# Seams between the seven stretches of a three-layer graph network: leaving without a drain, early zero stores, early first groups

## What is computed

```python
# attention (the edges of edge_index are the first 25,000 by shape only; here all 50,000 are used, plus a loop for each node)
xl = (x @ Wl); xr = (x @ Wr)
e = leaky_relu(xl[src] + xr[dst]); logits = einsum(e, att)
alpha = softmax of logits over the edges of a node
out = segment_sum(alpha * xl[src], dst) + bias
y = elu(graph norm of out over all nodes)
x = layernorm(x + y)
# two relational layers
for l in range(2):
    msg = sum_b comp[l, b][etype] * (h[src] @ basis[l, b])
    h = tanh(segment_sum(msg, dst) + h @ loop_w[l] + bias[l])
x = layernorm(x + h)
```

## Time and profile before

| | us |
|---|---|
| median of 3 runs | 3581.94 (3573.18 to 3585.92) |
| the profiled execution | 3583.63 |
| its span, first to last instruction | 3581.8 |
| busy: PE, DVE, POOL, ACT | 2957.1, 2565.8, 2222.8, 1815.4 |
| ends of the seven stretches in it | 1160.3, 1516.5, 1827.6, 2369.5, 2649.7, 3191.9, 3581.0 |

### The profile page before, as it was taken

One profiled execution on the slowest core, in us unless ns is written; L12 is line 12 of the kernel. 1 busy time (PEld: TensorE's weight loads), 2 busy tenths in 40 slices (PEclk: granted clock), 3 DMA queues, 4 the chain that ended last, 5 costly groups with the idle time before them and its releaser, 6 DMA issues. The chain is left out here.

```text
span 3581.8 us, 65764 instructions
## 1 busy us (share of the span) xinstructions
PE 2957.1 (83%) x17251; PEld 2212.4 (62%) x17251; DVE 2565.8 (72%) x8027; ACT 1815.4 (51%) x4346; POOL 2222.8 (62%) x2605
## 2 busy tenths in 40 slices
PE   4787888878775788788869999969979999967776
PEld 4777777777774555477745555548855555545654
DVE  4777777777775798877757777734447777758887
ACT  2444444444442344389956666634436666635554
POOL 6777777777773122278877777712247777726666
PEclk9899898999887899999989999989989999989998
DMA  4455555444442788678823333359943333349886
GB/s 100 121 127 124 123 123 129 124 121 128 122 123 71 210 247 245 193 258 271 270 92 104 103 103 104 105 166 301 299 150 104 103 103 104 104 143 291 280 281 202
DMA packets 647622, 579.28 MB, mean 162 GB/s; under 512 B 74323, under 2 KB 534484, under 8 KB 647252
## 3 DMA queue, kind: packets, MB, share of 16 engines
q1 hardware_dynamic: 494436, 335.02, 31.6%
q0 software_dynamic: 82688, 207.65, 20.9%
q10 hardware_dynamic: 70128, 32.39, 3.3%
HBM read 366.34 MB, written 208.43 MB: 160 GB/s over the span
## 5 line engine op out<-in xcount | busy, mean ns | idle before, releaser
L1867 DVE SCALAR_TENSOR_TENSOR work<-bank,coef,work 128x128 f32<-128x128 f32 x2400 | 673.9, 342 | 244.7 <-ACT work L1308 241.0
L1032 PE MATMUL bank<-basis_s,work 128*128 128x512 f32 x1600 | 755.9, 595 | 1.5 <-ACT work L1301 1.5
L744 POOL DMA_INDIRECT work<-in_x_dram,slot_src x400 | 423.4, 1059 | 130.9 <-issue 121.6
L744 POOL DMA_INDIRECT work<-in_x_dram,slot_dst x400 | 417.8, 1045 | 122.0 <-issue 122.0
L793 POOL DMA_INDIRECT work<-h_d,slot_src x400 | 384.4, 961 | 132.0 <-issue 121.7
L793 POOL DMA_INDIRECT work<-x_d,slot_src x400 | 383.9, 960 | 132.0 <-issue 121.7
L1308 ACT ACTIVATE work<-bank,coef 128x128 f32<-128x128 f32 x800 | 294.1, 368 | 224.7 <-PE bank L1032 224.7
L1032 PEld LDWEIGHTS bank<-basis_s,work 128*128 128x128 f32 x1600 | 274.3, 191 | 196.6 <-issue 192.6
L758 POOL DMA_DIRECT2D conv_d<-work x99 | 74.0, 751 | 325.3 <-DVE work L1756 315.9
L1078 PE MATMUL bank<-work,loop_s 128*128 128x512 f32 x392 | 213.8, 627 | 73.5 <-ACT work L1349 73.4
L1043 PEld LDWEIGHTS bank<-work 128*126 128x126 f32 x1600 | 206.9, 189 | 101.6 <-issue 100.9
(11 more groups left out here) (273 smaller groups left out, 7835.4 us busy)
## 6 DMA issues: line engine op xcount, KB each, us to landing
w_d<-work SPq DMA_DIRECT2D x800, 62.5 KB
work<-in_x_dram SPq DMA_DIRECT2D x194, 256.0 KB, 3.1
work<-x_d SPq DMA_DIRECT2D x194, 256.0 KB, 4.0
w_d<-work SPq DMA_DIRECT2D x400, 66.9 KB
work<-w_d SPq DMA_DIRECT2D x398, 64.0 KB, 3.2
work<-w_d ACTq DMA_DIRECT2D x390, 64.0 KB, 3.3
xl_d<-work SPq DMA_DIRECT2D x97, 256.0 KB
work<-xl_d SPq DMA_DIRECT2D x97, 256.0 KB, 3.8
```

The lines of the kernel that those rows point to most:

```text
L744: pool.indirect_dma_start(quad(k, i % 3)[:, c, :], None, x, bass.IndirectOffsetOnAxis(ap=table[:, a:a + 1], axis=0)).then_inc(e_in[i % 3], 16)
L1032: pe.matmul(psum[YBANKS[k % 5]][:, :], quad(1, i % 2)[:, c, :], basis_s[:, l, :, :].rearrange("k b n -> k (b n)"), start=True, stop=True). ...
L1867: ins = dve.scalar_tensor_tensor(o, psum[YBANKS[k % 5]][:, b * D:(b + 1) * D], coef[:, i, l, c, b:b + 1], o, ALU.mult, ALU.add)
```

## The change

- `end_pool_stage` takes the place of `end_stage` for POOL at all seven places: POOL adds one to `stage_done` without a drain.
- The zeros past the end are made and stored at the beginning of stretches 1, 4 and 6 from `work[15]`, not at the end from `work[6]`; the wait for them stands before the first store of sums.
- `node_at` is worked out before the first join and not after it.
- Own rows of node groups 0 to 2 are loaded at the beginning of stretches 4 and 6; PE turns group 0, ACT copies it and DVE makes the one-hot matrices 0 and 1 before the bridges, within the stretch of edges. In `update` the product with `loop_w` stands ahead of the wait for the packed sums.
- The first three groups of stretch 3 are loaded at the end of stretch 2, when all of its groups are merged (`skip_rows` swaps its two buffers for that), and ACT computes one Exp right after the Sqrt of the graph norm.
- PE's wait for the weights stands after the transposes of the slots.

```diff
+        def end_pool_stage(k):
+            pool = nc.gpsimd
+            pool.sem_inc(stage_done, 1)
+            pool.wait_ge(stage_done, 5 * k)
...
             def save_sums(i):
                 sp.wait_ge(ec_cp, i + 1)
+                if i == 0:
+                    sp.wait_ge(zero_out, 16)
...
+            sp.wait_ge(zero_ok, 1)
+            end = addresses(sp, end_at[0:1, 0:1])[0]
+            sp.dma_start(w_d[0][bass.ds(end, P), :], work[15][:, 0:WIDE]).then_inc(zero_out, 16)
             for i in range(ROWS + 3):
...
-            sp.wait_ge(zero_ok, 1)
-            at = addresses(sp, end_at[0:1, 0:1])[0]
-            sp.dma_start(w_d[0][bass.ds(at, P), :], work[6][:, 0:WIDE]).then_inc(zero_out, 16)
-            sp.wait_ge(zero_out, 16)
             for k, c in enumerate(range(CHAINS - 1, 0, -1)):
...
-            for q in range(QUADS):
+            sp.wait_ge(r["m_ps"], QUADS - 2)
+            sp.wait_ge(cv_ok, PAIRS)
+            for q in range(3):
+                sp.wait_ge(r["nh_out"][q], 16)
+                load_nx(q)
+            end_stage(sp, 2)
+
+            for q in range(3, QUADS):
                 load_nx(q)
...
+                sp.dma_start(w_d[l + 1][bass.ds(end, P), :], work[15][:, 0:width]).then_inc(r["zero_out"], 16)
...
+                for q in range(3):
+                    load_own_rows(q)
+                sp.wait_ge(r["zero_out"], was["zero_out"] + 16)
                 for i in range(ROWS):
...
-            end_stage(pool, 1)
+            end_pool_stage(1)
...
             pe.wait_ge(consts, 12)
-            pe.wait_ge(weights_in, 16 * 10)
...
+            pe.wait_ge(weights_in, 16 * 10)
             pe.wait_ge(pos_ok, 1)
...
                 compact(ROWS - 1)
+                pe.wait_ge(r["t_cp"], was["t_cp"] + ROWS)
+                turn_nodes(0)
                 end_stage(pe, 4 + 2 * l)
...
-                    wait_packed(pe, l, q)
                     if q >= 3:
                         pe.wait_ge(r["th_ok"], was["th_ok"] + q - 2)
                     pe.matmul(to[:, 0:m], loop_s[:, l, :], work[7][:, (q % 2) * 512:(q % 2) * 512 + m],
                               start=True, stop=False, skip_group_check=True)
+                    wait_packed(pe, l, q)
...
             act.activation(stat[:, 5, :], stat[:, 4, :], ACT.Sqrt).then_inc(gn_std, 1)
+            act.activation(join[:, 7, :], ones[0:1, 0:H], ACT.Exp)
             end_stage(act, 2)
...
+                turned_nodes(0)
+                end_stage(act, 4 + 2 * l)
...
-                dve.memset(work[6][:, 0:width], 0.0).then_inc(r["zero_ok"], 1)
+                node_matrix(l, 0)
+                node_matrix(l, 1)
                 dve.wait_ge(r["c_cp"], was["c_cp"] + ROWS)
```

More of the change, by code:

```diff
@@ L640, in _, with load_own_rows @@
                 was, width = counts_before(l), D
+                sp.wait_ge(r["zero_ok"], was["zero_ok"] + 1)
+                end = addresses(sp, end_at[0:1, 0:1])[0]
+                sp.dma_start(w_d[l + 1][bass.ds(end, P), :], work[15][:, 0:width]).then_inc(r["zero_out"], 16)
+                def load_own_rows(q):
+                    for to, part in run_rows((x1_d, h1_d)[l], q, h_rows(q), True):
+                        sp.dma_start(to, part).then_inc(r["n_in"][q % RING], 16)
+                for q in range(3):
+                    load_own_rows(q)
+                sp.wait_ge(r["zero_out"], was["zero_out"] + 16)
                 for i in range(ROWS):
@@ L649, in _ @@
                     sp.wait_ge(r["w_out"][c], was["w_out"][c] + 16 * ROWS)
-                sp.wait_ge(r["zero_ok"], was["zero_ok"] + 1)
-                at = addresses(sp, end_at[0:1, 0:1])[0]
-                sp.dma_start(w_d[l + 1][bass.ds(at, P), :], work[6][:, 0:width]).then_inc(r["zero_out"], 16)
-                sp.wait_ge(r["zero_out"], was["zero_out"] + 16)
                 for k, c in enumerate(range(CHAINS - 1, 0, -1)):
@@ L667, in load_group @@
                     load_packed(sp, l, q, 0, 2)
-                    for to, part in run_rows((x1_d, h1_d)[l], q, h_rows(q), True):
-                        sp.dma_start(to, part).then_inc(r["n_in"][q % RING], 16)
+                    if q >= 3:
+                        load_own_rows(q)
                 def load_skip(q):
@@ L1045, in compact, with turn_nodes @@
                     last.then_inc(r["c_ps"], 1)
+                def turn_nodes(q):
+                    wait_own(pe, l, q)
+                    if q >= 2:
+                        pe.wait_ge(r["nt_cp"], was["nt_cp"] + q - 1)
+                    for t in range(quad_tiles(q)):
+                        rows = tile_rows(4 * q + t)
+                        last = pe.transpose(psum[q % 2][:, t * P:t * P + rows], h_rows(q)[0:rows, t, :], ident[0:rows, 0:rows])
+                    last.then_inc(r["nt_ps"], 1)
                 turn(0)
@@ L1058, in _ @@
                 compact(ROWS - 1)
+                pe.wait_ge(r["t_cp"], was["t_cp"] + ROWS)
+                turn_nodes(0)
                 end_stage(pe, 4 + 2 * l)
-                def turn_nodes(q):
-                    wait_own(pe, l, q)
-                    if q >= 2:
-                        pe.wait_ge(r["nt_cp"], was["nt_cp"] + q - 1)
-                    for t in range(quad_tiles(q)):
-                        rows = tile_rows(4 * q + t)
-                        last = pe.transpose(psum[q % 2][:, t * P:t * P + rows], h_rows(q)[0:rows, t, :], ident[0:rows, 0:rows])
-                    last.then_inc(r["nt_ps"], 1)
                 def update(q):
@@ L1608, in hot_types @@
                 last.then_inc(hot_ok, 1)
+            dve.memset(work[15][:, 0:WIDE], 0.0).then_inc(zero_ok, 1)
             for i in range(ROWS + 1):
@@ L1628, in _ @@
             dve.wait_ge(ec_cp, ROWS)
-            dve.memset(work[6][:, 0:WIDE], 0.0).then_inc(zero_ok, 1)
+            dve.wait_ge(tile_in, 16 * 4)
+            less, kept = (work[k][:, 0:512].rearrange("p (g w) -> p g w", g=4)[:, :, 0:TE] for k in (0, 1))
+            node_f = work[7][:, 0:4]
+            st.did(dve.tensor_tensor(less, node_row[:, :, 0:TE], tile_base[:, :].unsqueeze(2).to_broadcast([P, 4, TE]), ALU.is_lt))
+            st.did(dve.tensor_tensor(kept[:, :, 1:TE], node_row[:, :, 1:TE], node_row[:, :, 0:TE - 1], ALU.not_equal))
+            st.did(dve.memset(kept[:, :, 0:1], 1.0))
+            st.wait()
+            st.did(dve.tensor_tensor(less, less, kept, ALU.mult))
+            st.wait()
+            st.did(dve.tensor_reduce(node_f, less, AX.X, ALU.add))
+            st.wait()
+            st.did(dve.tensor_tensor(node_f, node_f, node_row[:, :, TE], ALU.add))
+            st.wait()
+            regions = work[7][:, 4:16].rearrange("p (c g) -> p c g", c=CHAINS - 1)
+            for c in range(1, CHAINS):
+                st.did(dve.tensor_scalar(regions[:, c - 1, :], node_f, chain_at[:, c:c + 1], float(GAP), ALU.is_ge, ALU.mult))
+            st.wait()
+            for c in range(1, CHAINS):
+                to = node_f if c < CHAINS - 1 else node_at[:, :]
+                st.did(dve.tensor_tensor(to, node_f, regions[:, c - 1, :], ALU.add))
+                st.wait()
             for k, c in enumerate(range(CHAINS - 1, 0, -1)):
@@ L1873, in term @@
                         ins.then_inc(r["y_used"], 1)
+                dve.memset(work[15][:, 0:width], 0.0).then_inc(r["zero_ok"], 1)
                 for k in range(-1, TILES_E):
```

37 lines of the change are left out of this document (5 added, 32 removed).

## The result

| | us |
|---|---|
| kernel before, median of 4 runs beside it | 3583.93 (3573.18 to 3585.95) |
| changed kernel, median of 4 runs | 3545.7 (3543.07 to 3546.76) |
| ratio, with its interval | 0.9898 (0.9877 to 0.9919) |
| span of the profiled execution, before and after | 3581.8 and 3543.2 |

The change gives 38.2 us where 42.3 were forecast. A second set of runs gave 0.9899 (0.9881 to 0.9917). Ends of stretches are read to 0.1 us, so a piece is good to about 0.1 us.

A forecast was written before the change was run, and what follows sets the result against it. Seven successive stretches were taken as paced by POOL (1, 4, 6), ACT (3), PE (5) and DMA (7). Gains 3.6 + 4.5 + 5.5 + 16.2 + 4.1 + 5.6 + 2.8 = 42.3 us gave 3540 us, range 3528 to 3557.

The forecast's parts named there:

- Start, 3.6 us: Program start: PE turns the slots without waiting for the weights, so POOL's first gather and stretch 1's end come 3.6 us earlier.
- End of stretch 1, 4.5: End of stretch 1: no zero store before the bridges (2.3 us) and SP last instead of DVE (2.2), 4.5 us.
- Seam 2 to 3, 5.5: Stretch 3's start: early loads and early table load bring the first Exp 5.9 us forward, taken as 5.5; ACT keeps it.
- The drains, 16.2: Ends of stretches 3 and 5: without POOL's drain each stretch ends 8.1 us earlier, 16.2 us together.
- Rival B: POOL's queue pays the 8.1 us before the first gathers of stretches 4 and 6 anyway; 3556 us, chance 0.12.
- Start of stretch 5, 5.6: Stretch 5's start: group 0 prepared early, first squash (tanh) at 2376.4 against 2382.05; PE keeps the 5.6 us.
- Start of stretch 7, 2.8: Stretch 7's start: DMA engines set the pace and save three groups' own rows, 2.8 us, bounds 2 and 5.6.
- The end, 0: Program end: without POOL's last drain the program's own drain takes the 8.1 us instead, so 0 us gained.
- Rival A: Program end: the end drain goes too, saving another 8.1 us; 3532 us, chance 0.15.
- Rival C: Drains go, but half of what stretches 3, 5 and 7 gain at their starts, 7 us, is given back; 3547 us, chance 0.15.
- Rival D: Gathers of stretches 4 and 6 run at stretch 1's slower pace, 78 us more; 3618 us, chance 0.03.
- Rival E: Little effect: Rival B with starts absorbed and zero stores in a new wait, within 10.7 us of 3582; chance 0.03.

The follow-up runs named there:

- last_drain: The changed kernel with GpSimd's drain put back at the end of stretch 7 alone; 0.9933 of the kernel before.
- weights_only: The kernel before with only PE's wait for the ten weight loads moved behind the turning of the slot tables; 1.0013 of the kernel before.

## Why the prediction was right, point by point

- **Start, 3.6 us: wrong, 1.3.** The step that failed is "POOL's first gather follows". PE and the indices moved by 3.5 us, but POOL was held at the branch over the unsorted block; before the change this lay hidden behind the late transposes (9.2 us of idle time put down to `slot_dst` in the earlier trace rows). The trace showed a wait for `slot_dst`, and not what would be late next.
- **End of stretch 1, 4.5: right,** 4.6 in the profile, 5.3 when undone. **Ends of stretches 4 and 6, 4.1: right,** 3.9.
- **Seam 2 to 3, 5.5: right in kind.** The first Exp came 6.5 us earlier. How much stretch 3 kept can't be told: its inside took 292.2 us on average in the three kernels with the old start (290.0 to 294.8), and 294.9 in nine with the new one (289.1 to 303.7). Of 6.5 us 3.8 would stay by these means, with an uncertainty about as large as the difference. "ACT keeps what it is given" was too strong, since ACT also waits for stores to land, and that wait is not fixed. It was there before and had grown, as this group shows, in the kernel before (from 1530 to 1800) and in the changed one (from 1520 to 1790; busy us, mean ns, idle before):

```profile
L1281 ACT ACTIVATE work<-bank,norm 128x128 f32<-128x128 f32 x364 | 137.4, 464 | 16.5 <-DMA x_d<-work 16.3
...
L1302 ACT ACTIVATE work<-bank,norm 128x128 f32<-128x128 f32 x367 | 138.5, 463 | 21.0 <-DMA x_d<-work 20.0 <-issue 0.7 <-POOL norm L790 0.2
```

  The 20.0 us are 3.7 more than 16.3, most of the 4.5 that stretch 3 lost inside. That the early start makes the wait longer is not shown: over the whole stretch it was 18.4 us in `last_drain`, with the new start, and 18.5 in `weights_only`, with the old one.
- **The drains, 16.2: right,** 16.3 in the profile and 15.7 for all drains in the whole times. Rival B fell: POOL paid nothing ahead of its gathers, which begin 0.8 us after the stretch's end as before.
- **Start of stretch 5, 5.6: right,** first tanh 5.7 us earlier. "PE is the bound from there on and keeps it" failed in part: 2.0 us went inside in the profiled execution, in which PE worked 3.9 us longer at the half clock behind the first tanh, and 0.2 in the other. On average the inside took 258.4 us in four kernels with the old start and 259.5 in ten with the new one, so 4.6 of 5.7 us stayed.
- **Start of stretch 7, 2.8: right in kind, and near the lower bound of 2.** The first tanh came 4.5 us earlier, but not all of it stayed: 1.5 to 2.1 were lost when it was undone, and the insides (366.0 in four, 368.4 in ten) say 2.1. That it is the DMA engines that return the rest was not tested.
- **The end, 0: nearly right, -0.6.** The program's own drain took the place of the other, but 8.8 us and not 8.1. Rival A fell.
- **Rival C,** starts half absorbed, came in part, and the total does not decide against it: 3545.7 lies nearer to its 3547 than to the forecast's 3540. Stretch 3 at 300.9 stood above its mark of 300.2, stretch 5 at 268.3 below its own of 269.3. In the profile stretches 3, 5 and 7 gained 16.7 us at their starts and lost 7.4 of them inside; by the averages above 10.5 stayed, where the forecast had 13.9 and C 7.
- **Luck in the total.** The forecast was 3.7 us off in the profile, 0.2 at the edges and 3.5 inside. It would have been 7.3 off without the 3.6 us of stretch 1, which are scatter; the forecast's premise that stretch 1 ends a fixed time after its first gather does not hold to better than 9 us. For stretches 4 and 6 it held: 522.0 to 523.9 us from the first gather to the last sums in all six.
- **Rival D** fell: 960 and 962 ns for a gather in stretches 4 and 6. **Rival E** fell: 38.2 us are well above its 10.7.

**Open.** Why POOL's drain took 1.03 us behind the stores of stretch 2 and 8.13 behind those of stretches 3, 5 and 7. Whether instruction loading is what the branch costs; a shorter block was not tried. Whether stretches 3, 5 and 7 really run slower inside after an early start, or only scatter, and what part the clock has in it. A kernel that has the changed seams, the last stores on SP and no branch on POOL's path was not run; by the pieces, as an estimate (4.5 us at the end, 2.2 at the start), it would be some 7 us ahead of the changed one.

## What to carry to other kernels

Cut each stretch at events that both traces have, and compare the pieces: it gave each edit to some tenths of a microsecond where runs of one kernel lay 4 to 61 us apart. But an early start shows only at the edge: look inside the stretch, in several executions, for what is given back. In this program a drain on GpSimd was worth taking out only where GpSimd was last to leave; one was paid at the program's end in any case, and it could be started early by giving GpSimd's last work and waits to another engine. Before counting on an earlier start, ask for each engine what it did in the idle time that goes, a branch as much as a wait, and whether the work only moves to a time when TensorE has half its clock.

## What the hardware showed that I had not expected

- GpSimd's drain took 8127 to 8134 ns behind the stores of stretches 3, 5 and 7 in every kernel with drains in all stretches, 1034 behind those of stretch 2, 19 to 23 us behind gathers on the fast chip (11 to 21 on the one with 4005 us), and 8.7 to 9.6 us where no stretch before it had ended with one. Started beside stores in flight it was not shorter or longer by more than 0.8 us.
- A semaphore add behind waits was recorded with up to 2.8 us, and with 17 ns where nothing had to be waited for.
- Behind a branch over a block that is not entered GpSimd's next gather came 7.2 us after the reduction at the soonest; without block and branch it came at 15.37 us instead of 17.46 or later.
- The moment at which the granted clock rose from 0.50 to 1.00 in stretch 5 lay 7.1 us after its start in one execution and 11.7 in another of the same kernel.
- The same kernel took 3583, 3951 and 4005 us on three chips; by the profiles of its variants all of the difference lies in the stretches with gathers.
